# A selective scan with a mixture of experts beside it: the part ahead of the scan is put in another order

## The reference, cut to what matters

```python
x = L0_attn_x                       # (4, 1024, 256): 4 sequences, 1024 steps, 256 channels
xn = _layernorm(x, axis=-1)
# scan over 1024 steps, state h of (4, 256, 16)
dt = soft_clamp(softplus(xn @ Wdt.T + bdt), 0.001, 0.1, 0.5)      # soft_clamp: tanh(..) * r + c
A = -exp(soft_clamp(A_log, -5.0, 5.0, 0.5))
dA = exp(soft_clamp(dt[..., None] * A, -8.0, 8.0, 0.5))           # a tanh, then an exp, per state element and step
dB = dt[..., None] * (xn @ WB.T)[:, :, None, :]
def step(h, inp):
    h = dAt * h + dBt * xt[..., None]
    h = h * minimum(20.0 / (norm of h over channels and states + 1e-08), 1.0)
    y = einsum('bdn,bn->bd', h, Ct) + Dp * xt
# routing: each of 4096 tokens to 2 of 8 experts, at most 1280 tokens each
logits = xn @ w_g; top 2; probs = softmax of the two; rank = running count per expert
g = silu(sum over the token's experts of prob * (gelu(xn @ c_fc[e]) @ c_proj[e]))
out = x + ys * g
```

## Time and profile before

| | before |
|---|---|
| median of three runs | 1647.12 us (1644.81 to 1650.81) |
| the profiled execution: its time | 1646.17 us |
| its span, first to last instruction | 1644.4 us |
| DVE busy | 1532.7 us, 93% |
| first step of the scan starts at | 69.67 us |

### The profile page before, as it was taken

How to read it: one execution, slowest core, us unless ns; L and a number is a source line. 1 busy time by engine, 2 the same in 40 slices (tenths; PEclk the granted TensorE clock), 3 DMA queues, 4 the chain that set the end, 5 groups by cost and what they waited for, 6 DMA issues and landing times.

```text
span 1644.4 us, 34338 instructions
## 1 busy us (share of the span) xinstructions
PE 1282.0 (78%) x9628; PEld 1123.2 (68%) x9628; DVE 1532.7 (93%) x9635; ACT 1153.7 (70%) x2909; POOL 777.6 (47%) x1253
## 2 busy tenths in 40 slices
PE   5656445479989888989989998898989798855661
PEld 4445344368878777877978787797878688844550
DVE  7688888999999999999999999999999999987788
ACT  5877456486787768868776877778777777847450
POOL 5166776544444443444443344344444444468852
PEclk9776677789999999999989999999999999967895
DMA  9921111200111020111002002011100200012245
GB/s 319 315 83 50 42 44 43 98 15 30 43 49 43 16 75 22 36 62 37 30 16 87 23 25 73 24 37 41 57 22 24 66 30 17 17 39 73 73 149 194
DMA packets 85088, 104.56 MB, mean 64 GB/s; under 512 B 7712, under 2 KB 75936, under 8 KB 84896
## 3 DMA queue, kind: packets, MB, share of 16 engines
q1 hardware_dynamic: 76848, 85.47, 15.8%
q0 software_dynamic: 6144, 16.79, 3.2%
q10 hardware_dynamic: 1904, 0.09, 0.1%
HBM read 56.45 MB, written 45.88 MB: 62 GB/s over the span
## 4 chain that ended last, share of the span: by engine, by line
PE 48%; POOL 15%; ACT 14%; DVE 14%; issue 7%; DMA 2%; ACTq 0%; POOLq 0%; SPq 0%; DVEq 0%
PE ps L1219 15%; PE ps L1203 13%; PE ps L1191 8%; POOL arena L516 7%; PE ps L1185 5%; ACT arena L854 4%; POOL xg L496 4%; PE ps L1153 3%; DVE arena L724 2%; DVE arena L702 2%; DVE arena L718 2%; DVE arena L710 2%; DVE arena L696 2%; POOL wf L502 2%; PE ps L1069 2%
## 5 line engine op out<-in xcount | busy, mean ns | idle before, releaser
L516 POOL TENSOR_TENSOR arena<-arena,neghalf 128x1 f32<-128x1 f32 x1025 | 602.3, 588 | 798.4 <-DVE arena L699 751.1
L724 DVE SCALAR_TENSOR_TENSOR arena<-arena 128x128 f32<-128x128 f32 x1024 | 360.5, 352 | 23.5 <-POOL arena L516 23.5
L1191 PE MATMUL ps<-arena,pick 128*128 128x128 f32 x2048 | 301.9, 295 | 49.4 <-ACT arena L961 25.7
L1203 PE MATMUL ps<-arena,wf 128*128 128x256 f32 x1280 | 308.9, 393 | 20.3 <-ACT arena L974 9.4
L1191 PEld LDWEIGHTS ps<-arena,pick 128*128 128x128 f32 x2048 | 279.0, 210 | 62.8 <-ACT arena L961 50.1
L961 ACT ACTIVATE arena<-ps,arena 128x128 f32<-128x128 f32 x1024 | 292.3, 374 | 32.6 <-PE ps L1191 30.7
L710 DVE CUSTOM_DVE_ANT_0 arena<-arena 128x128 f32<-128x128 f32 x1024 | 293.3, 286 | 9.5 <-PE ps L1153 5.8
L702 DVE CUSTOM_DVE_ANT_0 arena<-arena 128x128 f32<-128x128 f32 x1024 | 299.1, 292 | 2.2
L1219 PE MATMUL ps<-wp,arena 128*128 128x256 f32 x1280 | 295.8, 385 | 3.1 <-ACT arena L974 3.1
L696 DVE TENSOR_TENSOR arena<-arena 128x128 f32<-128x128 f32 x1024 | 290.6, 284 | 0.0
L1203 PEld LDWEIGHTS ps<-arena,wf 128*128 128x128 f32 x1280 | 244.7, 198 | 53.5 <-ACT arena L974 10.2
(11 more groups left out here) (148 smaller groups left out, 1323.3 us busy)
## 6 DMA issues: line engine op xcount, KB each, us to landing
xg<-zeros SPq DMA_DIRECT2D x10, 1024.0 KB, 10.6
xrow<-xg SPq DMA_DIRECT2D x40, 256.0 KB, 2.7
yg<-arena SPq DMA_DIRECT2D x40, 256.0 KB, 2.1
arena<-in_x SPq DMA_DIRECT2D x16, 512.0 KB, 8.8
wf<-in_c_fc SPq DMA_DIRECT2D x8, 1024.0 KB, 5.1
wp<-in_c_proj SPq DMA_DIRECT2D x8, 1024.0 KB, 6.0
ys<-arena SPq DMA_DIRECT2D x66, 64.0 KB
xnd<-arena SPq DMA_DIRECT2D x8, 512.0 KB, 5.7
```

What stands on the lines that cost most here:

```text
L516: g.tensor_tensor(sv[:, slot, 1:2], mx, neghalf[:, 0:1], ALU.pow).then_inc(s_ready, 1)
L724: v.scalar_tensor_tensor(hr[:, slot, :], vv, sv[:, before, 1:2], ur[:, slot, :], ALU.mult, ALU.add)\
L1191: last = t.matmul(ps[2][:, j * P:(j + 1) * P], pick[:, q * QUAD + j, :], xin, start=True, stop=True)
L1203: last = t.matmul(ps[4 + j % 2][:, c * TS:(c + 1) * TS], wf[:, k, (2 * j + c) * P:(2 * j + c + 1) * P], xt[:, k, :], start=k == 0, stop=k ...
```

## The change

ACT zeroes the state ring `hr` and the window tile `win` instead of POOL. POOL's constants are counted in two parts, so that the first users wait for 12 only, and the selects of `pick` and of the others stand between POOL's powers. The small loads are in another order, with the one of A_log first. On PE and ACT the first half's `time_rates` and logarithms stand ahead of the second chunk. Before the scan ACT makes the Tanh of the first 16 steps alone (`tanh_part`, 32 instructions of 128x64, L866 of the changed kernel), and the other 48 steps (32 instructions of 128x192) in quads 0 to 2. DVE makes the ranks ahead of the probabilities. In the scan, `logs_of` is cut in two (`rates_out` and the rest) and its first part put ahead of two `decay_op`; `soft_clamp` stands in quad 9 of each half instead of behind quad 11; the third half's dt is made one block later; and the pieces of DVE's input product begin 3 steps later.

```diff
+CONSTS, CONSTS_A = 15, 12
-            for table, pieces, lo_, hi_ in ((input_at, PIECES, (4 * h - 6) * BLK + 10, (4 * h - 4) * BLK), ...
+            for table, pieces, lo_, hi_ in ((input_at, PIECES, (4 * h - 6) * BLK + 13, (4 * h - 4) * BLK), ...
...
-            g.memset(hr, 0.0).then_inc(h_ready, 1)
-            g.memset(win, 0.0).then_inc(init_win, 1)
...
             statistics(0)
-            for i in range(CH):
+            normalize(0)
+            statistics(1)
+            dve.wait_ge(a_exp, 1)
+            v.tensor_scalar(a16[:, :], alog, -DT_K / 16.0, None, ALU.mult).then_inc(a_ready, 1)
+            for i in range(1, CH):
...
+            act.wait_ge(memz, 1)
+            def clear_states(t):
+                return a.activation(hr[:, span(t, BLK), :], zeros[:, 0:P].unsqueeze(1).broadcast_to([P, BLK, P]), ACT.Copy)
+            clear_states(0)
+            act.wait_ge(ld_a, 16)
...
+            def tanh_part(first, count, t0, t1):
+                src = stage[:, 0, 0, :].rearrange("p (k b t) -> p b k t", b=NB, k=DH)
+                dst = tanhb[:, 0, :, :].rearrange("p (b k n) t -> p b k n t", b=NB, k=DH)
+                for c in range(first, first + count):
+                    k, n_ = divmod(c, NS)
+                    last = a.activation(dst[:, :, k, n_, t0:t1], src[:, :, k, t0:t1], ACT.Tanh, scale=a16[:, c:c + 1])
+                return last
...
             turned(0)
+            skip_of(0)
+            skip_of(1)
+            rates_out(0, PREP_BANKS[0])
+            logs_of(0)
+            turned(1)
+            clear_states(BLK).then_inc(h_ready, 1)
+            rates_out(1, PREP_BANKS[1])
+            logs_of(1)
+            logits_out(0)
+            turned(2)
+            act.wait_ge(consts, CONSTS_A)
+            soft_clamp(0)
...
+                    if quad < 3:
+                        last = tanh_part(11 * quad, min(11, 32 - 11 * quad), BLK, HALF)
...
+                        first, end = [32 * (c - 3) // 12 if blk < 4 else 32 * c // 15 for c in (quad % 16, quad % 16 + 1)]
+                    if blk % 4 == 2 and q == 1 and blk // 4 + 2 < HALVES:
+                        soft_clamp(blk // 4 + 2)
...
-                if blk % 4 == 2 and blk // 4 + 2 < HALVES:
-                    soft_clamp(blk // 4 + 2)
```

More of the change, by code:

```diff
@@ L50 @@
 PREP_BANKS = (4, 5)
-CONSTS = 17
+CONSTS, CONSTS_A = 15, 12
 PIECES = 16
@@ L206, in build @@
         consts = sem("consts")
+        picks = sem("picks")
+        ld_a = sem("ld_a")
+        rest_done = sem("rest_done")
         stat_chain = sem("stat_chain")
@@ L331, in build @@
         for h in range(2, HALVES):
-            for table, pieces, lo_, hi_ in ((input_at, PIECES, (4 * h - 6) * BLK + 10, (4 * h - 4) * BLK), (norm_at, 2, (4 * h - 2) * BLK, (4 * h - 1) * BLK)):
+            for table, pieces, lo_, hi_ in ((input_at, PIECES, (4 * h - 6) * BLK + 13, (4 * h - 4) * BLK), (norm_at, 2, (4 * h - 2) * BLK, (4 * h - 1) * BLK)):
                 free_ = [k for k in delayed if lo_ <= k < hi_ and k not in input_at and k not in norm_at]
@@ L460, in _ @@
             made(g.memset(ones[:, :], 1.0))
-            made(g.memset(pick[:, :, :], 0.0))
+            g.memset(pick[:, :, :], 0.0).then_inc(picks, 1)
             made(g.memset(bsum[:, :], 0.5))
@@ L490, in _ @@
                 g.tensor_tensor(rs[:, :, i], vare[:, i, :], neghalf[:, :], ALU.pow).then_inc(rstd_ready, 1)
+                if i == 1:
+                    made(g.affine_select(out=q4, in_=q4, compare_op=ALU.is_ge, fill=0.0, base=0,
+                                         pattern=[[-32, NB], [0, 32]], channel_multiplier=1))
+                    made(g.affine_select(out=lows, in_=lows, compare_op=ALU.is_gt, fill=0.0, base=0,
+                                         pattern=[[1, P]], channel_multiplier=-1))
+                    pool.wait_ge(consts, CONSTS_A + 1)
+                    made(g.affine_select(out=q4, in_=q4, compare_op=ALU.is_ge, fill=0.0, base=31,
+                                         pattern=[[32, NB], [0, 32]], channel_multiplier=-1))
+                    assert n[0] == CONSTS, n[0]
+                if 2 <= i < 6:
+                    pk = pick[:, span((i - 2) * QUAD, QUAD), :].rearrange("p t (g n) -> p t g n", g=NG)
+                    if i == 2:
+                        pool.wait_ge(picks, 1)
+                    g.affine_select(out=pk, in_=pk, compare_op=ALU.not_equal, fill=1.0, base=-NG * QUAD * (i - 2),
+                                    pattern=[[-NG, QUAD], [-1, NG], [0, NS]], channel_multiplier=1).then_inc(picks, 1)
             def send(n):
@@ L801, in logs_of @@
                 last.then_inc(z_used, 1)
+            def logs_of(h):
+                flat = stage[:, h % 2, 0, :]
                 act.wait_ge(z_used, h + 1)
@@ L856, in _ @@
             turned(0)
[L857 to L868, removed]
+            act.wait_ge(ld_v, 32)
+            act.wait_ge(xt_sb, 1)
+            a.activation(bdt_sb, bdt_sb, ACT.Copy, scale=-1.0, bias=Z_TOP).then_inc(act_chain, 1)
             skip_of(0)
             skip_of(1)
-            turned(5)
-            logits_out(4)
+            act.wait_ge(act_chain, 1)
+            rates_out(0, PREP_BANKS[0])
[7 more added lines that the diff above has]
+            act.wait_ge(consts, CONSTS_A)
             soft_clamp(0)
+            turned(3)
+            logits_out(1)
             soft_clamp(1)
-            turned(6)
-            logits_out(5)
+            turned(4)
+            logits_out(2)
             act.wait_ge(a_ready, 1)
             act.wait_ge(th_ready, 1)
-            tanh_ops(0, 0, 4)
+            tanh_part(0, 4, 0, BLK)
+            turned(5)
+            logits_out(3)
+            b_and_c_out(0, PREP_BANKS[0])
+            turned(6)
+            logits_out(4)
+            b_and_c_out(1, PREP_BANKS[1])
             turned(7)
+            logits_out(5)
             logits_out(6)
@@ L883, in _ @@
             squares_of(0)
-            tanh_ops(0, 4, 4)
+            tanh_part(4, 6, 0, BLK)
             squares_of(1)
-            tanh_ops(0, 8, 4)
+            tanh_part(10, 6, 0, BLK)
             sums_out(0, PREP_BANKS[0])
             sums_out(1, PREP_BANKS[1])
-            tanh_ops(0, 12, 20).then_inc(tanh_done, 1)
+            tanh_part(16, 16, 0, BLK).then_inc(tanh_done, 1)
+            a.activation(win.rearrange("p t c g -> p (t c g)").rearrange("p (a b) -> p a b", a=2),
+                         zeros[:, 0:BLK * NG * WIN // 2].unsqueeze(1).broadcast_to([P, 2, BLK * NG * WIN // 2]), ACT.Copy).then_inc(win_ready, 1)
             act.wait_ge(tanh_done, 1)
@@ L963, in _ @@
                     last.then_inc(u_done, 1)
+                    if blk % 4 == 0 and 0 < blk and q == 0 and blk // 4 + 2 < HALVES:
+                        rates_out(blk // 4 + 2, 6)
                     if blk % 4 == 0 and 0 < blk and q == 0:
@@ L998, in _ @@
                         inputs_out_of_psum(blk + 1)
-                    if blk + 4 < NBLK and quad % 16 < 15:
-                        if blk % 4 == 0 and q == 0:
+                    if quad < 3:
+                        last = tanh_part(11 * quad, min(11, 32 - 11 * quad), BLK, HALF)
+                        if quad == 2:
+                            last.then_inc(rest_done, 1)
+                            act.wait_ge(rest_done, 1)
+                    elif blk + 4 < NBLK and quad % 16 < 15:
+                        if (blk % 4 == 0 and q == 0) or quad == 3:
                             act.wait_ge(th_ready, blk // 4 + 2)
@@ L1005, in _ @@
                                 act.wait_ge(xn_out, 16 * CH)
-                        first = 32 * (quad % 16) // 15
-                        last = tanh_ops(1 - f, first, 32 * (quad % 16 + 1) // 15 - first)
+                        first, end = [32 * (c - 3) // 12 if blk < 4 else 32 * c // 15 for c in (quad % 16, quad % 16 + 1)]
+                        last = tanh_ops(1 - f, first, end - first)
                         if quad % 16 == 14:
@@ L1093, in _ @@
             turn(0)
+            pe.wait_ge(xt_sb, 1)
+            pe.wait_ge(ld_w, 80)
+            time_rates(0, PREP_BANKS[0])
+            turn(1)
+            time_rates(1, PREP_BANKS[1])
             for i in range(CH):
                 pe.wait_ge(xt_sb, i + 1)
-                if i + 1 < CH:
+                if 1 <= i < CH - 1:
                     turn(i + 1)
-                if i == 0:
-                    time_rates(0, PREP_BANKS[0])
-                    time_rates(1, PREP_BANKS[1])
                 if i in (2, 3):
@@ L1224, in _ @@
                     h = {(3, 3): blk // 4 + 3, (0, 1): blk // 4 + 2, (1, 0): blk // 4 + 1}.get((blk % 4, q), 0)
-                    if blk == 0:
-                        h = {1: 2, 2: 2}.get(q, 0)
+                    if blk < 2:
+                        h = {5: 2, 6: 2}.get(quad, 0)
                     if 2 <= h < HALVES:
@@ L1230, in _ @@
                         after_evictions()
-                        if blk % 4 == 3 or (blk == 0 and q == 1):
```

(3 more changed lines are left out.)

54 lines of the change are left out of this document (19 added, 35 removed).

## The result

The changed kernel takes 1631.67 us (median of five, 1625.10 to 1633.83) against 1649.29 us (five runs of before on the same chip): ratio 0.9889, 95% interval 0.9873 to 0.9904. That is 17.6 us or 1.1% less, where 12.7 us was forecast; 1631.67 us lies in the range. The execution that was profiled took 1625.1 us, the fastest of the five, so its span, 1623.4 us, shows more gain than the median does: 21.0 us against the 1644.4 us of before.

What follows compares the result with a forecast made beforehand. DVE, busy 93% of the span, was taken to bound the kernel. Start 11.9 us, less 0.7 debt and 0.5 sends, plus 2.0 inside the scan made 12.7 us, so 1634.5 us; range 1629.5 to 1642.

Steps and rivals of the forecast that it cites:

- Start of the scan: DVE's work ahead of the scan: first step at 57.8 us instead of 69.67, a gain of 11.9 us.
- logits: Ahead of the scan: last chunk ends at 39.3 us, logits reach DVE at 41.6 us, 5.4 us earlier.
- ACT's `ur`: ACT's chain beside DVE's at the start: first `ur` out at 57.1 us, 0.7 us ahead of DVE.
- The debt in the first quads: ACT's remaining Tanh, 11.0 us in quads 1 to 3: 0.7 us of DVE stall, between 0 and 5.
- Transfers: SP and DMAs: eight clears start at 44.4 us, 3.7 earlier; ACT's wait for the stored output ends at 85.2.
- The sends: POOL's sends early in the scan: one may meet the loads' backlog, costing 0.5 us, between 0 and 3.
- Inside the scan: DVE's waits in the scan: both on `soft_clamp` go; gain 2.0 us, between +3.8 and a loss of 3.
- Rival E: `soft_clamp` in quad 9 delays quad 10's evictions in 14 later halves: slower, 1654 us at full cost; chance 0.04.

Runs made afterwards that it cites:

- e1: Changed kernel with early Relu, `soft_clamp` in quad 9 and later input pieces all undone, leaving the front only; 1638.80 us, ratio 0.9933 to the kernel before.
- e8: Changed kernel with the Tanh of all 64 steps made whole ahead of the scan, none in the first three quads; 1630.79 us, ratio 0.9884 to before.
- e2: Kernel before with only the three scan edits: early Relu, earlier `soft_clamp`, later input pieces; 1637.38 us, ratio 0.9936.
- e9: Kernel before with one edit, the Relu of the next half's dt ahead of the two decay Exps; 1639.54 us, ratio 0.9951.
- e4: Changed kernel with `soft_clamp` behind quad 11 again and input pieces from step 42 again; 1626.15 us, ratio 0.9848 to before.
- e6: e4 with the zeroing of the state ring's second half moved ahead of ACT's first chunk; 1625.93 us, ratio 0.9852 to before.
- e10: Changed kernel with DVE's input pieces from step 42 of a half again, `soft_clamp` staying in quad 9; 1629.12 us, ratio 0.9878 to before.
- e5: Changed kernel timed again, unaltered; 1632.10 us, ratio 0.9898 to before.
- e7: Changed kernel with the three probability instructions and their wait ahead of the ranks again; 1631.20 us, ratio 0.9886 to before.

## Why the prediction was right where it was, and what failed

**Start of the scan.** Right, term by term: logits at 41.29 (41.6 forecast), first step at 57.26 (57.8), ACT's `ur` at 56.54 (57.1). The prediction's own terms, 39.3 us and 2 us more, give 41.3 us for the logits and not the 41.6 written; the slip put the first step 0.3 us late. e1 prices the whole front at 11.0 us (10.7 forecast).

**The debt in the first quads.** The waits are 0.36 us at step 11 and 0.23 at step 19 (0.7 and nothing forecast; step 19 was put at 88.2 us, where 57.8 + 29.2 + 0.5 is 87.5, so its margin was 0.5 us and not 1.2). The mechanism held: e8, without the debt, has neither.

**Transfers.** The eight clears start at 44.45 us (44.4 forecast), and ACT's wait for the output ends at 85.39 (85.2). The sends were under-sized: the third waits 1.61 us for the one before it, where I had 0.5 us in all:

```profile
90.86 1.04 POOL L503 DMA_INDIRECT xg<-wf,slot_of  x1 [1.61 <-DMA xg<-wf,slot_of]
```

Together the two terms were 1.2 us. Between the first step and step 128 the changed kernel loses 12.4 - 10.7 = 1.7 us.

**Inside the scan.** This is the step that was off: "I take a gain of 2.0 us, between +3.8 and a loss of 3". I read DVE's waits only, took the two on `soft_clamp` as what the edits remove, and let the other 9.4 us stand "since ACT and PE come no earlier". The Relu's new place had no term at all. But PE does come earlier: its own waits, which the sum left out, show 16.2 us behind the Relu, and the early Relu takes 13 of them away. e2 measured 10.5 us for the three edits on the old front, e9 8.1 us for the Relu alone. In the changed kernel 17.6 - 11.0 = 6.6 us of it are left.

**Luck.** That the time lies in the range is partly luck. The early Relu gave about 13 us over e1, which the prediction did not have, and the other two edits took about 6 us of it back, which it had only as a rival at 0.04. Without them (e4) the time is 1626.15 us, under the range's lower end of 1629.5.

**Rival E**, that `soft_clamp` in quad 9 costs time, had 0.04 and a price of 14 to 20 us. Its sign seems right on the new front, at about 6 us (e4, e6, e10), but its reason, waits for quad 10, is not in the traces.

The fastest kernels here are e4 and e6, the change without the `soft_clamp` part: 1626 us, 0.4% under the changed one.

## What to carry to other kernels

Where the critical engine waits for another, ask next what that other engine waits for: an instruction that only frees a buffer belongs ahead of long work on its queue, even if nobody on the critical engine names it. A start that is made earlier is worth what the next arrival allows; here an output's transfer at 85 us took back most of a start that was 1.9 us earlier still (e6). And put each edit of a bundle back alone: one of these took its wait away and, by the times, still cost some.

## What the runs showed of the hardware that was not expected

Executions of one binary differ by 5 to 11 us (changed kernel: 1624.8 to 1635.9 us in e5), and profiles fall into patterns. Here is DVE's wait at step 576 in e7, e8 and e10. From quad 3 on their scans differ in the place of e10's pieces alone; their fronts differ by the edits above. The line it waits for (L1192, L1189 in e8) is PE's matmuls of y, which read the states that DVE is about to write over:

```profile
926.86 0.29 DVE L714 CUSTOM_DVE_ANT_0 arena<-arena 128x128 f32<-128x128 f32 x1 [1.30 <-PE ps L1192]
```

```profile
929.47 0.29 DVE L714 CUSTOM_DVE_ANT_0 arena<-arena 128x128 f32<-128x128 f32 x1 [1.29 <-PE ps L1189]
```

```profile
924.52 0.29 DVE L714 CUSTOM_DVE_ANT_0 arena<-arena 128x128 f32<-128x128 f32 x1 [1.30 <-PE ps L1192]
```

All three wait at steps 451, 527, 528, 543, 576, 579, 643, 655, 656, 835 and 839; of these, the changed kernel's profiles have only 643 and 656. e2, with the old front, waits at the first nine of these steps too. The granted clock goes with the pattern: its mean from step 512 to step 576 is 0.93 in e2, e7, e8 and e10, and 0.97 to 0.98 in e9, which has none of these waits, and in the changed kernel's three profiles. But it is 0.93 in e4 too, which of these steps waits only at 543, 643 and 656. Whether a lower clock makes the waits or the waits a lower clock, no run here shows.

From 300 to 1500 us DVE waits 10.1 us for ACT and PE in e7 and e10, and 1.4 to 2.3 us in the changed kernel's profiles. So single profiles of such kernels can differ by over 5 us for no edit's sake, and the verdicts here rest on medians and intervals.
